# Attention stage: the mask added by VectorE instead of by mask matmuls, two turned heads copied by ScalarE, and a new order of steps

## What is computed

```python
xn = layernorm(x)
q = (xn @ Wq + bq).reshape(bs, n, 8, 32)      # k and v in the same way
logits = einsum('bqhd,bkhd->bhqk', q, k) / sqrt(32)
logits = where(adj > 0, logits, -1e9)
attn = softmax(logits, axis=-1)
out = relu(einsum('bhqk,bkhd->bqhd', attn, v).reshape(bs, n, 256) @ Wo + bo)
x = x + out
```

## Time and profile before

| | |
|---|---|
| median of the runs | 3056.38 us |
| profiled execution | 3055.62 us |
| its span | 3053.8 us |
| mean granted TensorE clock over the span | 0.966 |
| TensorE matmul busy | 2739.7 us (90%) |
| ScalarE busy | 1762.0 us (58%) |
| VectorE busy | 1689.3 us (55%) |
| GpSimd busy | 1499.9 us (49%) |

### The profile page before, as it was taken

One profiled execution on the slowest core, in us unless ns is written; L12 is line 12 of the kernel. 1 busy time (PEld: TensorE's weight loads), 2 busy tenths in 40 slices (PEclk: granted clock), 3 DMA queues, 4 the chain that ended last, 5 costly groups with the idle time before them and its releaser, 6 DMA issues. The chain is left out here.

```text
span 3053.8 us, 112957 instructions
## 1 busy us (share of the span) xinstructions
PE 2739.7 (90%) x42816; PEld 2402.5 (79%) x42816; DVE 1689.3 (55%) x5612; ACT 1762.0 (58%) x4802; POOL 1499.9 (49%) x2680
## 2 busy tenths in 40 slices
PE   6999999968888888859999999999999999999944
PEld 5777777757777777758988988999999899999922
DVE  5777777734444444445666664444444445444469
ACT  4666666644444444436766765666666577777711
POOL 5666666620000000036666665555555566666643
PEclk9999999989999999979999999999999999999965
DMA  2111111000000000020000011000000100000002
GB/s 87 37 39 35 34 34 34 21 7 13 13 12 13 13 13 12 13 73 22 26 25 21 26 32 33 23 9 9 9 7 9 30 9 9 9 7 8 9 31 82
DMA packets 110487, 72.32 MB, mean 24 GB/s; under 512 B 51424, under 2 KB 109280, under 8 KB 110432
## 3 DMA queue, kind: packets, MB, share of 16 engines
q1 hardware_dynamic: 96464, 58.93, 6.7%
q10 hardware_dynamic: 13968, 12.72, 1.4%
HBM read 50.63 MB, written 20.97 MB: 23 GB/s over the span
## 5 line engine op out<-in xcount | busy, mean ns | idle before, releaser
L1462 PE MATMUL g_F<-g_w,g_act 128*128 128x256 f32 x3072 | 698.2, 381 | 0.0
L1462 PEld LDWEIGHTS g_F<-g_w,g_act 128*128 128x128 f32 x3072 | 578.4, 191 | 75.1
L1445 PE MATMUL g_H<-g_hT_upper,g_w_upper 128*128 128x256 f32 x1536 | 442.3, 288 | 0.0
L1445 PE MATMUL g_H<-g_hT_upper,g_w_rest 128*128 128x256 f32 x1536 | 434.7, 283 | 0.0
L1445 PE MATMUL g_H<-g_hT_rest,g_w_upper 128*128 128x256 f32 x1536 | 434.3, 283 | 0.0
L744 POOL COPY l_xt<-seq 128x64 f32 x256 | 60.9, 238 | 597.4 <-PE l_O L755 595.7
L328 ACT ACTIVATE a_probs<-a_S,a_nmax 128x256 f32<-128x256 f32 x512 | 236.8, 481 | 127.9 <-DVE a_nmax L421 95.0
L1102 ACT ACTIVATE g_act<-g_H,g_small 128x256 f32<-128x256 f32 x768 | 291.4, 490 | 5.5 <-PE g_H L1445 4.4
L1445 PEld LDWEIGHTS g_H<-g_hT_upper,g_w_upper 128*128 128x128 f32 x1536 | 294.2, 192 | 0.1
L1445 PEld LDWEIGHTS g_H<-g_hT_rest,g_w_upper 128*128 128x128 f32 x1536 | 294.1, 191 | 0.0
L1445 PEld LDWEIGHTS g_H<-g_hT_upper,g_w_rest 128*128 128x128 f32 x1536 | 294.0, 191 | 0.0
(11 more groups left out here) (203 smaller groups left out, 7088.6 us busy)
## 6 DMA issues: line engine op xcount, KB each, us to landing
gmask<-masks ACTq DMA_DIRECT2D x97, 128.0 KB, 2.0
x<-in_x_dram SPq DMA_DIRECT2D x32, 256.0 KB, 3.0
a_adj<-in_adj_dram SPq DMA_DIRECT2D x32, 256.0 KB, 2.8
hidden<-l_hs SPq DMA_DIRECT2D x512, 16.0 KB, 1.4
g_hs<-hidden SPq DMA_DIRECT2D x32, 256.0 KB, 2.7
out_dram<-q_res SPq DMA_DIRECT2D x32, 256.0 KB, 2.1
g_w<-in_L_gnn_W_dram SPq DMA_DIRECT2D x6, 1024.0 KB, 6.3
masks<-gmask SPq DMA_DIRECT2D x32, 128.0 KB, 1.7
```

Source lines behind the costliest of these rows:

```text
L1445: last = pe.matmul(hidden_bank[m // 2][:, m % 2 * N:(m % 2 + 1) * N], w[:, c, m * P:(m + 1) * P], x[:, c, :], start=(c == 0 and k == 0), s ...
L1462: last = pe.matmul(ff_bank[:, it * D:(it + 1) * D], act1[:, m, it * P:(it + 1) * P], w2[:, m, :], start=(m == 0 and it == 0), stop=(m == M ...
```

## The change

- `masks` writes +1e30 where there is no edge, and waits for the row extremes (`max_done`) of the graph two back in place of its scores, since VectorE now reads the mask. The queries are made with the scale -1/sqrt(32), so the scores come out negated.
- `cover` is gone, all eight per graph and the four ahead of the first. `scores` start afresh (`start=True`).
- `largest` becomes `smallest`: two `tensor_tensor_reduce` of 128 x 256 per head. Each reads half a score bank and the bf16 mask, writes the sum back in place into PSUM, and gives the row minimum as a second output. `exponent` takes scale -1.
- Heads 1 and 5 are copied by ScalarE (`late_out`) instead of VectorE (`early_out`). The semaphore counts are 2 early and 6 late copies per graph.
- `k_out` signals each of its two halves; `scores(b, 0)` wants only the first. `weigh` waits for both halves before it turns the spread reciprocals into `in_bank`.
- New orders. GpSimd: `norm2` ahead of `masks`. VectorE: `v_out`, `heads_out`, `moments1` in place of `moments1`, `heads_out`, `early_out(b, 1)`, `v_out`; `q_out` ahead of `early_out(b, 4)`. TensorE: `values` between turns 0 and 1 instead of behind turn 1; `queries` ahead of turn 4 and `keys` behind turn 5 instead of behind turns 4 and 6. ScalarE: `late_out(b, 1)` behind exponent 2, `late_out(b, 5)` behind exponent 6.

```diff
-                    pool.tensor_scalar(mask[i][:, :], adj[...], 0.0, MASKED,
+                    pool.tensor_scalar(mask[i][:, :], adj[...], 0.0, -MASKED,
...
+                    if exists(b - 2):
+                        norm2(b - 2)
                     if exists(b + 1):
                         masks(b + 1, 1 - i)
-                    if exists(b - 2):
-                        norm2(b - 2)
...
-                                              ACT.Exp, bias=nmax[:, h, it:it + 1], accum_out=den[:, h, it:it + 1])
+                                              ACT.Exp, bias=nmax[:, h, it:it + 1], scale=-1.0,
+                                              accum_out=den[:, h, it:it + 1])
...
                     exponent(b, 2)
+                    late_out(b, 1)
                     exponent(b, 3)
...
-                    for h in range(HG, H):
+                    for h in range(HG, H - 1):
                         exponent(b, h)
+                    late_out(b, 5)
+                    exponent(b, H - 1)
...
-                def largest(b, h):
-                    dve.wait_ge(scores_ps, b * H + h + 1)
-                    dve.tensor_reduce(nmax[:, h, :], score_bank[h % HG][:, :].rearrange("p (t k) -> p t k", t=NT), AX.X,
-                                      ALU.max, negate=True).then_inc(max_done, 1)
+                def smallest(b, h, i):
+                    if h == 0:
+                        dve.wait_ge(mask_done, b + 1)
+                    alone(dve, scores_ps, b * H + h + 1, passed)
+                    for it in range(NT):
+                        part = score_bank[h % HG][:, it * N:(it + 1) * N]
+                        last = dve.tensor_tensor_reduce(out=part, in0=part, in1=mask[i][:, it * N:(it + 1) * N], scale=1.0,
+                                                        scalar=3.0e38, op0=ALU.add, op1=ALU.min,
+                                                        accum_out=nmax[:, h, it:it + 1])
+                    last.then_inc(max_done, 1)
...
                     for h in range(HG):
-                        largest(b, h)
+                        smallest(b, h, i)
                     early_out(b, 0)
+                    v_out(b)
+                    if exists(b - 1):
+                        heads_out(b - 1)
                     if exists(b + 2):
                         moments1(b + 2)
-                    if exists(b - 1):
-                        heads_out(b - 1)
-                    early_out(b, 1)
-                    v_out(b)
...
-                def cover(b, h, i):
-                    if h == 0:
-                        pe.wait_ge(mask_done, b + 1)
-                    pe.matmul(score_bank[h % HG][:, :], t.identb[:, :], mask[i][:, :], start=True, stop=False, skip_group_check=True)
-
                 def scores(b, g):
-                    if g == 0:
-                        pe.wait_ge(k_done, b + 1)
+                    pe.wait_ge(k_done, b * KC + g + 1)
...
                     pe.wait_ge(spread_done, b + 1)
+                    pe.wait_ge(k_done, (min(b + 2, B) if isinstance(b, int) else b + 2) * KC)
...
-                    for h in range(2):
-                        turn_probs(b, h)
-                        cover(b, h + HG, i)
+                    turn_probs(b, 0)
                     values(b)
+                    turn_probs(b, 1)
                     turn_probs(b, 2)
-                    cover(b, 2 + HG, i)
...
                     turn_probs(b, 3)
-                    cover(b, 3 + HG, i)
                     scores(b, 1)
                     if exists(b - 1):
                         project(b - 1)
-                    for j in range(HG):
-                        turn_probs(b, HG + j)
-                        if exists(b + 1):
-                            cover(b + 1, j, 1 - i)
-                            if j == 0:
-                                queries(b + 1)
-                            if j == 2:
-                                keys(b + 1)
+                    if exists(b + 1):
+                        queries(b + 1)
+                    turn_probs(b, 4)
+                    turn_probs(b, 5)
+                    if exists(b + 1):
+                        keys(b + 1)
+                    turn_probs(b, 6)
+                    turn_probs(b, 7)
```

More of the change, by code:

```diff
@@ L142, in attention_phase @@
         proj_ps, gated_done, x_done = sem("proj_ps"), sem("gated_done"), sem("x_done")
+        EARLY, LATE = 2, 6
         passed, pool_passed = sem("passed"), sem("pool_passed")
@@ L243, in masks @@
                 def masks(b, i):
-                    after(pool, scores_ps, (b - 1) * H)
+                    after(pool, max_done, (b - 1) * H)
                     alone(pool, adj_in, b * 16 + 16, pool_passed)
-                    pool.tensor_scalar(mask[i][:, :], adj[:, :, :].rearrange("p t n -> p (t n)"), 0.0, MASKED,
+                    pool.tensor_scalar(mask[i][:, :], adj[:, :, :].rearrange("p t n -> p (t n)"), 0.0, -MASKED,
                                        ALU.is_le, ALU.mult).then_inc(mask_done, 1)
@@ L408, in k_out @@
                     for c in range(KC):
-                        last = dve.tensor_scalar(kT[:, c, :], in_bank[:, c * N:(c + 1) * N], bk_col[:, c:c + 1], None, ALU.add)
-                    last.then_inc(k_done, 1)
+                        dve.tensor_scalar(kT[:, c, :], in_bank[:, c * N:(c + 1) * N], bk_col[:, c:c + 1], None,
+                                          ALU.add).then_inc(k_done, 1)
                 def v_out(b):
@@ L479, in graph @@
                     for h in range(HG, H):
-                        largest(b, h)
+                        smallest(b, h, i)
                     if exists(b - 1):
                         gate(b - 1)
-                    early_out(b, 4)
                     if exists(b + 1):
                         q_out(b + 1)
+                    early_out(b, 4)
                     if exists(b - 1):
                         residual(b - 1)
-                    early_out(b, 5)
                     if exists(b + 1):
@@ L496, in _ @@
                 dve.wait_ge(rows_in, 4 * 16)
-                dve.memset(qscale[:, :], HD ** -0.5)
-                dve.tensor_scalar(bqs_col[:, :], bq_col[:, :], HD ** -0.5, None, ALU.mult).then_inc(bqs_done, 1)
+                dve.memset(qscale[:, :], -HD ** -0.5)
+                dve.tensor_scalar(bqs_col[:, :], bq_col[:, :], -HD ** -0.5, None, ALU.mult).then_inc(bqs_done, 1)
                 moments1(1)
@@ L591, in scores @@
                             last = pe.matmul(score_bank[j][:, it * N:(it + 1) * N], qT[o:o + HD, g, it * P:(it + 1) * P],
-                                             kT[o:o + HD, g, :], start=False, stop=True, skip_group_check=True)
+                                             kT[o:o + HD, g, :], start=True, stop=True, skip_group_check=True)
                             if it == NT - 1:
@@ L597, in turn_probs @@
                     pe.wait_ge(probs_done, b * H + h + 1)
-                    if h % HG < 2:
-                        after(pe, late_done, b * (H // 2) + h // HG * 2 + h % 2 - 1)
+                    if h % HG == 2:
+                        pe.wait_ge(early_done, b * EARLY + h // HG + 1)
                     else:
-                        pe.wait_ge(early_done, b * (H // 2) + h // HG * 2 + h % 2 + 1)
+                        after(pe, late_done, b * LATE + {0: -1, 1: 0, 3: 1, 4: 2, 5: 3, 7: 4}[h])
                     for kt in range(NT):
@@ L608, in weigh @@
                 def weigh(b):
-                    pe.wait_ge(late_done, (b + 1) * (H // 2))
-                    pe.wait_ge(early_done, (b + 1) * (H // 2))
+                    pe.wait_ge(late_done, (b + 1) * LATE)
+                    pe.wait_ge(early_done, (b + 1) * EARLY)
                     pe.wait_ge(v_done, b + 1)
@@ L668, in _ @@
                 keys(0)
-                for j in range(HG):
-                    cover(0, j, 0)
                 walk(pe, graph)
```

## The result

The changed kernel takes 3037.56 us (median of 4 runs, 3035.99 to 3037.94) against 3056.20 us before: a ratio of 0.9936, 95% interval 0.9919 to 0.9953. It is 18.6 us faster; the forecast was 35 us, with a range down to 9 us. The time lies outside the forecast's own band of 3014 to 3030 us and inside the one of the first rival, 3030 to 3050, which had been given 0.17.

What follows compares the result with a forecast made beforehand. A closed loop of waits, not a full engine, bounds the kernel: 18.50 us a graph, forecast 17.36 (-1.14). Thirty graphs -34.2 and start -1 give 3055.6 - 35.2 = 3020.4, so 3021 us; range 3011 to 3047.

Steps and rivals of the forecast that it cites:

- the first rival: Dearer extreme: PSUM write makes a VectorE half cost 0.455 us, loop 18.23 us, total 3047 us; chance 0.17.
- The loop before: Waits from one moments2 on VectorE to the next, through norm2, TensorE and ScalarE, sum to 18.50 us a graph.
- norm2 ahead of masks: GpSimd: takes masks' 2.03 us out of the loop; norm2 gets slack; most of the saving was credited to it.
- The extreme: VectorE's masked row extreme: two halves at 0.35 us, 0.70 a head against 0.60; 0.85 until ScalarE starts exp.
- The crossing: Extreme's cost per head, near 0.75 us (a half of 0.37), where 13.7 + 5 s meets 16.66 + s.
- the second loop: Loop through the second group of extremes, four heads and gate to q_out: 13.7 + 5 s, s us a head.
- its mark: Sign of the dearer extreme: halves over 0.37 us apart, and q_out follows gate on VectorE without a gap.
- The estimate that was set aside: Skill page's 120 cycles plus one per element at 0.96 GHz, PSUM source: 0.39 us a half, some 7 us slower.
- Covers: TensorE: eight at 0.22 us, 1.7 us a graph; only two lay in the loop, the rest becomes idle time.
- Copies: Heads 1 and 5: VectorE gives 2 x 0.60 us, ScalarE takes 2 x 0.49; turn 7 ready just in time.
- k_out in halves and the start: scores(b, 0) start 0.4 us earlier, little kept; without the first four covers about 1 us is saved once.
- The slower rival: VectorE's halves don't overlap: 0.62 us each, 20.2 us a graph, total 3107 us; chance 0.07.

Runs made afterwards that it cites:

- b_norm2: The kernel before with only norm2 moved ahead of masks on GpSimd: 3035.48 us, ratio 0.9940 to before.
- a_norm2: The changed kernel with norm2 behind masks again on GpSimd: 3036.92 us, ratio 0.9943 to the kernel before.
- a_cover: The changed kernel with the mask back on TensorE (covers, one 512-element reduction per head): 3029.25 us, ratio 0.9912 to the kernel before.
- a_cover_vh: The changed kernel with covers and 512-element reductions, values behind turn 1, heads_out ahead of v_out: 3001.14 us, ratio 0.9821 to the kernel before.
- a_vhg: The changed kernel, mask on VectorE, with values behind turn 1, heads_out ahead of v_out, gate behind q_out: 3001.03 us, ratio 0.9822 to the kernel before.
- a_gnn_psum: The changed kernel with the graph network's tensor_tensor_reduce also writing in place into PSUM, exp reading there, TensorE waiting for exp: 3036.91 us, one run.
- a_rden: The changed kernel with rden_out ahead of exponent(b, 1) instead of behind it on ScalarE: 3016.01 us, ratio 0.9873 to the kernel before.

## Why the prediction was right, and where its size was off

*The loop before.* Right. b_norm2 fell by the amount that the removal of masks' 2.03 us from it, with the next loop taking over, was expected to give (20.4 us, 21 expected), and the wait for norm2 went. One link is open: turn 4 starts at 318.27 right behind `project` with no idle time, so the way from scores(b, 1) to turn 4 may be TensorE's own work (1.15 + 1.81) and not the maximum and exp of head 4 (1.16 + 1.80). The sum is the same.

*norm2 ahead of masks, "most comes from norm2's move".* The mechanism was right, the sharing out was not. In the changed kernel the move is worth nothing (a_norm2), for the new order puts a wait for heads_out at the same place. A share of a gain belongs to a part only in one order of undoing.

*The extreme, and the steps around it.* The loop came out at 17.87 us where 17.36 was forecast. The extreme was mis-sized: 0.70 us a head taken, 0.76 measured (0.38 a half). The crossing stood at 0.75 a head, so the second loop, in which a head counts five times, took over. Against its own forecast of 13.7 + 5 x 0.70 = 17.2, measured 17.87: 0.3 for five heads at 0.06 more, 0.15 for the first extreme of the second group (1.31 behind scores against 1.16), 0.07 more until exp 0 (0.98 against 0.85, less the head's 0.06), 0.09 ahead of the first extreme (0.26 against 0.17), 0.11 for heads_out until turn_xn2 (0.83 against 0.72). Nothing else moved by more than 0.04.

The takeover is the smaller part of the miss. Of the 0.51 us between 17.36 and 17.87 it is worth 0.15, the lead of the second loop in the rows. The other 0.36 lie in steps that both loops share: 0.06 for the extreme ahead of exp 0, and the 0.07, 0.09 and 0.11 above, with 0.03 in small ones. The first rival named the mechanism and its mark, and both are in the rows. Its price does not cover the result: it had 3047 us for 0.455 a half, and for the measured 0.38 its formula gives 13.7 + 3.8 = 17.5, one us a graph less than before, 3025 us. The other 12 us up to 3037.6 are the waits around the extremes and the one for heads_out, which the forecast had too small. That 3037.6 falls into this rival's band is in part luck: a half 0.075 us cheaper than it said, and waits that it did not have.

*The estimate that was set aside.* The Trainium skill, page "VectorE: DVE Perf Modes", section on the TRN2 errata, had given an estimate of 0.39 a half, which I set aside for the row of 0.35. The page's row is for PSUM read and SBUF written. For that case the changed kernel's graph network shows 0.35 again, so the trace still disagrees with it; the 0.38 came with the output in PSUM, for which the page has no row, and that it lies near 0.39 confirms nothing. Had the estimate been taken, the forecast was 3028. The rule of the page "Advanced Engine Details and Errata" of the Trainium skill, section "The Read-Write Bubble", that latency shows between instructions and large tiles keep it small, fits: two halves 0.76, one reduction of 512 0.60. But the halves also add the mask and write PSUM, so this is no clean test of it.

*Covers.* Their 1.7 us a graph are gone and leave TensorE idle, as said. That they bring nothing is shown by a_cover in the changed kernel's order and by the tie of a_cover_vh and a_vhg in the better one.

*Copies.* "Cost" was right, their part was missed: the prediction took them as work moved, but the new order depends on them. Alone 0, undone 20.5 us.

*k_out in halves and the start.* The first scores start at 25.16 instead of 26.69 (1.5 saved, 1 said), but graph 0 is 0.6 longer (43.36 - 25.16 against 44.27 - 26.69). The second figure need not be the change's: a_gnn_psum, the same attention in another execution, has 42.84 - 25.54 = 17.3 where the changed kernel has 18.2. The first holds on average: 25.0 over seven executions without covers, 26.5 over five with them. The halves of k_out were not tried apart.

*The slower rival* wanted the halves not to overlap. They do: the accumulator read begins with the next half.

Left open: what the two sequencer steps ahead of the first extreme (a wait and an increment by themselves) cost. The 0.15 and 0.09 us stand behind them in the rows, but a kernel without them was not run. The 0.09 may as well come from the scores: the first extreme starts 1.34 us behind scores(b, 0) at 296.89, much as in the second group (1.31). In the next graph, where the scores are out earlier, the first extreme stands 0.36 behind the reciprocal (316.29 to 316.65), against the 0.17 of the kernel before.

## What to carry to other kernels

Find the closed loop of waits first and price a change in it; then name the next loop and its distance, here 0.05 us a head, since part of a gain can end there. Price the waits around a new instruction too: here the forecast missed more on them than on the instruction. Undo each part in the changed kernel and do it alone in the old one: a step can be worth 20 us in one and nothing in the other. And when work is moved behind a wait (values behind rden_out, heads_out behind v_out), look at that wait before the engine's load. Taking both such moves back, with gate behind q_out (a_vhg), was worth 36.5 us, twice the whole change; one step of ScalarE moved (a_rden) was worth 21.6.

## What was not expected of the hardware

Tensor_tensor_reduces of 128 x 256 that write to PSUM and stand behind one another take 0.38 us each from start to start against 0.35 with the output in SBUF, and the accumulator read takes 0.14 us against 0.08. This holds in both stages, with bf16 as second operand in one and fp32 in the other. The first of such a row takes 0.35. The gate behind the last one is not longer than before the change: its successor starts 0.60 behind it, as there.

And kernels with TensorE at 99% and at 96% both took 3001 us, the one with an engine nearly full, the other with a loop of waits.
